# Moving ScalarE's high parts, tanh and gate exponential ahead of its reads of the round's own units

## Chip, cores and metric

The kernel runs on one core of a Trainium2 chip. The metric is device time in microseconds of one execution; lower is better. Times come from runs on the chip, and the trace from one further, profiled execution.

## What is computed

The input `x` has 8 sequences of 512 tokens with 256 features. After a layer norm (`xn`), three branches are computed and all are added to `x`:

```python
xn = layernorm(x)
# branch 1: state-space block
u  = causal_conv4(xn @ W_in + b_in)          # depthwise, 4 taps, 512 channels
ys = scan(h = tanh(A) h + u_t Bp;  y = Cp h + Dp u_t)
r1 = silu(ys) @ W_out + b_out
# branch 2: attention, 16 heads of 16, softmax over 512 keys
r2 = softmax(q k^T / 4) v
# branch 3: mixture of 8 experts, the two largest gates
r3 = sum_e combine_e * (xn @ W_e + b_e)
out = x + r1 + r2 + r3
```

The scan is linear and the same for every channel, so the kernel replaces it with a product along time by a Toeplitz matrix of the impulse response (`Rh`, `Rl`), done ahead of `W_in`. `silu(y)` is computed as `y/2 * (1 + tanh(y/2))`.

## The kernel before, in words

**Numbers in two parts.** Every matrix product is made of single-pass fp32r operands. A value is split into a high part, which ScalarE writes (a copy that rounds to fp32r), and a low part, which VectorE or GpSimd writes as value minus high part. A product is then three matmuls: high by high, low by high, high by low (`three`, L464).

**Rounds.** The main loop has one round `t` for each score tile: 256 rounds with scores (8 sequences, 4 groups of heads each, 8 tiles a group), and 16 more to drain. In round t:

- TensorE (`@block.tensor`, loop at its end) does `score(t)` (L591) into `SB`; `turned(t - 11)` (L608), the transposed scores, into `TB`; in each fourth round `values(m)` (L624); and then the units that the planner gave to this round (`AT[t]`).
- VectorE does `largest(t)` (L1051), the row maximum of `SB`; then the convolution taps (`conv`, L897 for the first tap and L901 for the other three); then the low parts of the units that are read in this round; then `(tanh + 1) * ys` (L1086); then a few gate steps and layer-norm steps (`xn`, L1027).
- ScalarE does the exponential of `TB` (L830), and reads the units out of PSUM.
- GpSimd adds the results in `mt` to `acc` (L1118) and makes the low parts `yl` (L1239) and `xl` (L1216).

`score(t)` waits for `largest(t - 1)`, since there is one `SB`. Each engine runs its own list in the order in which it is written; semaphores alone join the lists.

**Units.** A unit is a batch of matmuls into one of three PSUM banks (`FB`): T transposes `xn`, V makes values and gate logits, Q makes queries and keys, Z is the Toeplitz product, Y is the product with `W_in`, M is an expert product, O is the product with `W_out`, C and X are small transposes, P transposes the attention output for the normalisation. `plan()` sets the order when the kernel is built, from a table of TensorE costs (`COST`), a table of VectorE work (`VECTOR`) and due times (`WANTED`). All engines follow that plan. Of the units that TensorE computes in round t, the last is read by the other engines at the beginning of round t + 1 (`early(t + 1)`), and all others at the end of round t itself (`late(t)`). A bank is taken again three units later, when both reads of it are over.

**ScalarE's round.** The list of ScalarE (`@block.scalar`, the loop over t from -1) is: reads of `early(t)`, the exponential of `TB`, every eighth round a copy of the attention output, reads of `late(t)`, and then these four items, when the round has them:

```python
for b, d in y_read(t - 6): y_hi(b, d)     # L761: yh <- th
for b, d in y_read(t - 4): tanh(b, d)     # L753: th <- ys
x_hi(b, t - XH[b])                        # L767: xh <- xn
G[:, 1] = exp(G[:, 0])                    # L870: the gate's exponential
```

Their waits are: `y_hi` for L1086 of the round before, and for an O unit of the sequence before; `tanh` for all four taps of its convolution (the last tap is done by VectorE in this same round t, right behind `largest(t)`) and for `yl` of the Y unit before, on GpSimd, since `th` is one buffer; `x_hi` for its part of `xn`; the gate's exponential for a subtraction on GpSimd. The four items are 32 + 32 + 32 + 8 = 104 instructions in the whole program.

VectorE's list in round t has the low part of a unit in `late(t)` right behind the taps: for a Q unit `qkl` (L927) waits until ScalarE has written `qkh` (L704); for a V unit the gate logits (L922) wait until ScalarE has written `V` (L694); for a T unit `xTl` (L914) waits for `xTh` (L690); for an X unit `ml` (L909) waits for `mh` (L685).

Of the kernel before, what the change touches and what calls it, by code (L numbers as in the profile page):

```python
# [9 lines left out]
ACT = mybir.ActivationFunctionType  # L10
AX = mybir.AxisListType

NB = 8
# [158 lines left out]
AT, XH, LN = plan()  # L172
# [13 lines left out]
def gate_at(t, engine):  # L186

    for b in range(NB):
        for name, on, late in GATE:
            if on == engine and UNIT["V", b, 3].t + 1 + late == t:  # L190
                yield b, name


def early(t):

    return AT[t - 1][-1:] if t - 1 in AT else []


def late(t):

    return AT[t][:-1] if t in AT else []
# [7 lines left out]
def gate_count(b, name):  # L209

    mine = [n for n, on, _ in GATE if on == ON[name]]
    return b * len(mine) + mine.index(name) + 1


def y_read(t):

    return [(u.b, u.i) for u in early(t) + late(t) if u.kind == "Y"]


def program(nc, x, wqk, bqk, wqk0, bqk0, wvg, bv, bg, win, bin_, cw, cwt, cb, A, AT_, Bp, Cp, Dp, wout, bout, wexp, bexp, out):  # L220
    ctx = ExitStack()
    with ctx:
        def sb(name, shape, dt=F32):
            return ctx.enter_context(nc.sbuf_tensor(name, shape, dt))

        def sem(name):
            return ctx.enter_context(nc.semaphore(name))
# [72 lines left out]
        G = sb("G", [128, 6, 4, 8])  # L300
# [68 lines left out]
        s_gate = {"DVE": sem("gate_vector"), "POOL": sem("gate_pool"), "ACT": sem("gate_scalar")}  # L369
# [27 lines left out]
        def full(kind, b, i):  # L397
            u = UNIT[kind, b, i]
            return s_full[u.bank], u.use
# [8 lines left out]
        def gate_done(b, name):  # L408
            return s_gate[ON[name]], gate_count(b, name)
# [29 lines left out]
        def shifted_rows(e, k, s):  # L439

            p = (0, 64, 8, 72, 16, 80, 24, 88)[k]
            src = kp[p:p + 1, :]
            e.dma_start(Rraw[16 * k:16 * k + 16, :],
                        bass.AP(src.tensor, src.offset + 128 - 16 * k, [[src.ap[0][0], 1], [-1, 16], [1, 640]])).then_inc(s, 16)
# [7 lines left out]
        def turned_bank(t):  # L452

            return SB if t >= FREE and (t - FREE) % 2 == 0 else TB
# [207 lines left out]
        def _(e):  # L662
            def split(w):
                stg, src, hi, lo, sc = stages[w]
                e.wait_ge(s_w[w], 16)
                e.activation(hi, stg, ACT.Copy, scale=sc).then_inc(s_hi[w], 1)
# [79 lines left out]
            def tanh(b, d):  # L746
                n = 4 * b + d
                e.wait_ge(s_cv, 4 * n + 4)
                if n:
                    e.wait_ge(s_yl, n)  # L750
                else:
                    e.wait_ge(s_kr, 1)
                e.activation(th[:, :], ys[:, d % 2, :], ACT.Tanh, scale=0.5).then_inc(s_th, 1)  # L753

            def y_hi(b, d):
                e.wait_ge(s_y, 4 * b + d + 1)
                if b:
                    e.wait_ge(*full("O", b - 1, d // 2 * 2 + 1))
                elif d == 0:
                    e.wait_ge(*full("B", 0, 3))  # L760
                e.copy(yh[:, d, :], th[:, :]).then_inc(s_yh, 1)  # L761

            def x_hi(b, a):
                e.wait_ge(s_xn, 4 * b + a + 1)
                if b and a == 0:
                    e.wait_ge(*full("Y", b - 1, 3))
                e.copy(xhn[:, a, :], xn[:, a, :]).then_inc(s_xh, 1)  # L767

            def krylov(s):
                P = TB[:, s % 2, :]  # L770
                m = 1 << s
                e.wait_ge(s_kx, s + 1)
                if s < 8:
                    e.copy(Pm[:, (s + 1) % 2, :], P[0:17, 256:290]).then_inc(s_kv, 1)
                e.copy(V0[:, m:2 * m], P[0:17, 0:m]).then_inc(s_kv, 1)

            def at_start(t):
                if t == 0:
                    split(W_E0)
                elif t == 1:  # L780
                    e.wait_ge(s_bw, 2)
                    e.copy(bst, bwr).then_inc(s_wh, 1)
                    split(W_E1)
                elif t == 2:
                    e.wait_ge(s_rr[0], 64)
                    e.wait_ge(s_rr[1], 64)
                    e.copy(Rh[:, :], Rraw).then_inc(s_Rh, 1)
                    e.wait_ge(s_srs, 48)
                    e.copy(sst[0:68, :], sraw).then_inc(s_sh, 1)
                elif t == 3:  # L790
                    split(W_IN)
                elif t == 4:
                    split(W_E2)
                elif t == 5:
                    split(W_E3)
                elif t == 8:
                    e.wait_ge(s_br, 48)
                    e.copy(bhi, braw).then_inc(s_bh, 1)
                elif t == 12:
                    split(W_OUT)  # L800
# [17 lines left out]
            for t in range(-1, END + 1):  # L818
                for u in early(t):
                    unit(u)  # L820
                    for s in KRYLOV.get((u.kind, u.i), ()) if t == 0 else ():
                        krylov(s)
                T = t - LAG
                if 0 <= T < STEPS:
                    e.wait_ge(s_ST, T + 1)
                    if T >= NP:
                        e.wait_ge(s_PV, (T - NP) // 2 + 1)
                    elif T < 3:
                        e.wait_ge(s_lo[(W_Q0, W_VG, W_IN)[T]], 1)
                    e.activation(Pt[:, T % NP, :, :], turned_bank(T)[:, :, :], ACT.Exp, scale=0.25).then_inc(s_ex, 1)  # L830
                g, rest = divmod(t - LAG - 8, 8)
                if rest == 0 and 0 <= g < NG:
                    e.wait_ge(s_PV, 4 * g + 4)
                    if g:
                        e.wait_ge(*full("P", (g - 1) // 4, g - 1))
                    else:
                        e.wait_ge(s_kr, 1)
                    e.copy(ot[:, :], OB[:, :]).then_inc(s_ot, 1)
                for u in late(t):
                    unit(u)  # L840
                    if t == -1:
                        for s in KRYLOV.get((u.kind, u.i), ()):
                            krylov(s)
                        if (u.kind, u.i) == ("T", 1):
                            split(W_VG)
                            split(W_QK)
                    if t == 0 and (u.kind, u.i) == ("V", 0):
                        krylov(8)
                    if t == 0 and (u.kind, u.i) == ("V", 1):
                        e.wait_ge(s_kr, 1)  # L850
                        e.wait_ge(s_id, 3)
                        e.copy(kp[:, 256:768], TB[:, 1, :]).then_inc(s_kp, 1)
                        e.wait_ge(s_kp, 1)
                        e.wait_ge(s_c[C_DP], 16)
                        for p in (slice(0, 32), slice(64, 96)):
                            e.activation(kp[p, 256:257], kp[p, 256:257], ACT.Identity,
                                         bias=dpc[p, :]).then_inc(s_kp, 1)
                        e.wait_ge(s_kp, 3)
                        for k in range(4, 8):
                            shifted_rows(e, k, s_rr[1])  # L860
                for b, d in y_read(t - 6):
                    y_hi(b, d)
                for b, d in y_read(t - 4):
                    tanh(b, d)
                for b in range(NB):
                    if 0 <= t - XH[b] < 4:
                        x_hi(b, t - XH[b])
                for b, name in gate_at(t, "ACT"):
                    e.wait_ge(*gate_done(b, "s"))
                    e.activation(G[:, 1, :, :], G[:, 0, :, :], ACT.Exp).then_inc(s_gate["ACT"], 1)  # L870
                at_start(t)

        @block.vector
# [495 lines left out]
```

## Time and profile before

| what | value |
|---|---|
| median of 3 runs | 788.62 us (787.76 to 788.94) |
| the profiled execution, its own time | 787.89 us |
| span of the profiled execution | 786.1 us |
| time of that execution outside its span | 1.8 us |
| mean granted TensorE clock | 0.994 |
| rounds | 256 with scores, 16 to drain |

Times in the rows below are us from the start of the span. A row of a timeline is: start, length, engine, line, operation, operands, number of instructions merged into it, and in brackets the idle time of the engine just before it with the instruction that ended it. ScalarE is ACT, VectorE is DVE, GpSimd is POOL, TensorE's matmuls are PE and its weight loads PEld.

### The profile page before, as it was taken

The numbers are of one execution on the slowest core, as the hardware profiler recorded it, in microseconds if no ns is written. First come the engines' busy times: TensorE is split into PE (matmuls) and PEld (weight loads), VectorE is DVE, ScalarE is ACT, GpSimd is POOL, SyncE is SP. The second block draws the span as 40 slices with busy tenths as digits, with TensorE's granted clock in tenths as the row PEclk, the third lists the DMA queues.
The fourth block names the chain that finished last, engine by engine and source line by source line (L and its number), as shares of the span: only waits on it lengthen the run. The fifth ranks groups of instructions, "written<-read, shape, count | busy, mean of one in ns | idle before, by whom it ended". The sixth has DMA issues, their size and how long they took to land.

```text
span 786.1 us, 13228 instructions
## 1 busy us (share of the span) xinstructions
PE 753.9 (96%) x4404; PEld 453.3 (58%) x4404; DVE 581.4 (74%) x846; ACT 535.4 (68%) x926; POOL 387.4 (49%) x522
## 2 busy tenths in 40 slices
PE   9689999999998999999999999989999999999996
PEld 7457556565555655556555665556655565555553
DVE  6689876976679875887759876698667987568920
ACT  4637766777666767667567775667666776767775
POOL 8445554455444834456346463445444473435654
PEclk9989999999999999999999999999999999999999
DMA  8301201122110221102111121113111121112000
GB/s 272 69 4 44 68 19 28 38 59 78 35 38 13 79 58 41 42 22 82 35 42 42 45 82 31 38 25 95 42 42 43 32 58 39 46 41 69 23 2 27
DMA packets 32465, 39.09 MB, mean 50 GB/s; under 512 B 8513, under 2 KB 18535, under 8 KB 32398
## 3 DMA queue, kind: packets, MB, share of 16 engines
q1 hardware_dynamic: 31418, 37.29, 18.1%
q10 hardware_dynamic: 980, 0.96, 0.6%
q8 instruction: 35, 0.57, 0.3%
q14 instruction: 32, 0.26, 0.1%
HBM read 8.74 MB, written 4.19 MB: 16 GB/s over the span
## 4 chain that ended last, share of the span: by engine, by line
PE 80%; DVE 13%; issue 4%; ACT 3%; ACTq 0%; DVEq 0%
PE PS L464 39%; PE PS L624 12%; PE SB L591 12%; PE TB L608 7%; PE PS L521 5%; DVE mx L1051 4%; PE PS L480 2%; DVE ys L901 2%; DVE xn L1027 1%; PE PS L631 1%; DVE xl L933 1%; DVE qkl L927 1%; DVE ys L897 1%; PE PS L476 1%; DVE th L1086 1%
## 5 line engine op out<-in xcount | busy, mean ns | idle before, releaser
L1051 DVE TENSOR_REDUCE mx<-SB 128x2 f32<-128x1024 f32 x256 | 312.9, 1222 | 141.0 <-PE SB L591 139.9
L1118 POOL TENSOR_TENSOR acc<-acc,mt 128x256 f32<-128x256 f32 x320 | 247.9, 782 | 251.0 <-ACT mt L675 178.9
L830 ACT ACTIVATE Pt<-TB 128x1024 f32<-128x1024 f32 x251 | 257.7, 1027 | 59.3 <-PE TB L608 56.3
L675 ACT ACTIVATE mt<-PS,cpad 128x256 f32<-128x256 f32 x256 | 107.5, 471 | 58.9 <-PE PS L464 58.5
L591 PE MATMUL SB<-kst,qst 48*128 48x512 f32 x512 | 127.9, 496 | 14.6 <-DVE mx L1051 14.3
L624 PE MATMUL PS<-Pt,V 128*17 128x512 f32 x1024 | 122.3, 595 | 0.0
L591 PEld LDWEIGHTS SB<-kst,qst 48*128 48x128 f32 x512 | 47.7, 183 | 125.3 <-DVE mx L1051 75.1
L464 PE MATMUL PS<-weh,xTh 128*128 128x512 f32 x256 | 109.9, 429 | 2.2 <-DVE xTl L914 1.3
L608 PE MATMUL TB<-qst,kst 50*128 50x512 f32 x502 | 101.2, 398 | 1.1 <-ACT Pt L830 1.0
L464 PE MATMUL PS<-wel,xTh 128*128 128x512 f32 x256 | 100.9, 394 | 0.0
L464 PE MATMUL PS<-weh,xTl 128*128 128x512 f32 x256 | 100.6, 393 | 0.0
L901 DVE SCALAR_TENSOR_TENSOR ys<-uc,cwc,ys 128x511 f32<-128x511 f32 (+2 forms) x96 | 88.3, 919 | 0.0
L464 PEld LDWEIGHTS PS<-weh,xTh 128*128 128x128 f32 x256 | 48.4, 189 | 29.2 <-issue 15.8
L624 PEld LDWEIGHTS PS<-Pt,V 128*17 128x17 f32 x1024 | 23.5, 96 | 62.9 <-issue 62.6
L1239 POOL TENSOR_TENSOR yl<-th,yh 128x512 fp32r<-128x512 f32 x32 | 42.1, 1316 | 32.2 <-ACT yh L761 32.1
L464 PEld LDWEIGHTS PS<-wel,xTh 128*128 128x128 f32 x256 | 48.1, 188 | 11.1
L464 PEld LDWEIGHTS PS<-weh,xTl 128*128 128x128 f32 x256 | 48.4, 189 | 6.9
L608 PEld LDWEIGHTS TB<-qst,kst 50*128 50x128 f32 x502 | 47.7, 187 | 5.5 <-ACT Pt L830 5.0
L1216 POOL TENSOR_TENSOR xl<-xn,xh 128x256 fp32r<-128x256 f32 x32 | 28.8, 906 | 20.6 <-ACT xh L767 20.6
L1127 POOL TENSOR_TENSOR acc<-acc,at 128x256 f32<-128x256 f32 x31 | 24.5, 789 | 29.1 <-DVE at L961 27.7
L464 PE MATMUL PS<-wouth,yh 128*128 128x256 f32 x128 | 37.3, 291 | 0.0
L464 PE MATMUL PS<-woutl,yh 128*128 128x256 f32 x128 | 36.0, 281 | 0.0
(162 smaller groups left out, 1142.6 us busy)
## 6 DMA issues: line engine op xcount, KB each, us to landing
qst<-qkh SPq DMA_DIRECT2D x124, 64.0 KB, 2.3
kst<-qkh SPq DMA_DIRECT2D x124, 64.0 KB, 2.3
out<-acc SPq DMA_DIRECT2D x8, 512.0 KB, 2.8
qst<-qkl SPq DMA_DIRECT2D x62, 64.0 KB, 2.2
kst<-qkl SPq DMA_DIRECT2D x62, 64.0 KB, 2.3
acc<-in_x SPq DMA_DIRECT2D x7, 512.0 KB, 3.9
Bt<-in_wexp SPq DMA_DIRECT2D x2, 512.0 KB, 7.6
raw<-in_wexp SPq DMA_DIRECT2D x2, 512.0 KB, 8.8
```

The lines of the kernel that those rows point to most:

```text
L464: ins = e.matmul(P, u, v, start=(start and k == 0), stop=(stop and k == n - 1))
L521: ins = e.matmul(P[:, lo:lo + n], p[:, c, fs], q[:, r:r + n], start=(k == 0), stop=(k == 11))
L591: ins = e.matmul(SB[:, h, :], qst[rows, g % 3, jj, 128 * a:128 * a + 128], kst[rows, g % 3, jj, :], start=True, stop=True)
L608: ins = e.matmul(turned_bank(t)[:, h, :], kst[rows, g % 3, jj, 128 * a:128 * a + 128], qst[rows, g % 3, jj, :], start=True, stop=True)
L624: ins = e.matmul(OB[32 * j:32 * j + 17, :], V[:, g // 4 % 2, a, 4 * (g % 4) + j, :], Pt[:, (2 * m + j % 2) % NP, j // 2, :], start=(a == 0 ...
L675: return e.activation(mt[:, item % NM, :], P, ACT.Copy, scale=scale)
L830: e.activation(Pt[:, T % NP, :, :], turned_bank(T)[:, :, :], ACT.Exp, scale=0.25).then_inc(s_ex, 1)
L901: ins = e.scalar_tensor_tensor(out=y[:, s:512], in0=v[:, 0:512 - s], scalar=cwc[:, d, 3 - s:4 - s], in1=y[:, s:512], op0=ALU.mult, op1=ALU ...
L1051: e.tensor_reduce(mx[:, g % 2, 0:2, 4 * jj + a], SB[:, :, :], AX.X, ALU.max).then_inc(s_mx, 1)
L1118: e.tensor_tensor(v, v, mt[:, item % NM, :], ALU.add).then_inc(s_mt, 1)
L1216: e.tensor_tensor(xln[:, a, :], xn[:, a, :], F(xhn[:, a, :]), ALU.subtract).then_inc(s_xl, 1)
L1239: e.tensor_tensor(yl[:, d, :], th[:, :], F(yh[:, d, :]), ALU.subtract).then_inc(s_yl, 1)
```

## The change

In the loop of ScalarE the four items move ahead of the reads of `late(t)`. They still stand behind the exponential of `TB` and the copy of the attention output. Nothing is added or taken away; no other engine's list changes, and the plan is the same.

```diff
                     e.copy(ot[:, :], OB[:, :]).then_inc(s_ot, 1)
+                for b, d in y_read(t - 6):
+                    y_hi(b, d)
+                for b, d in y_read(t - 4):
+                    tanh(b, d)
+                for b in range(NB):
+                    if 0 <= t - XH[b] < 4:
+                        x_hi(b, t - XH[b])
+                for b, name in gate_at(t, "ACT"):
+                    e.wait_ge(*gate_done(b, "s"))
+                    e.activation(G[:, 1, :, :], G[:, 0, :, :], ACT.Exp).then_inc(s_gate["ACT"], 1)
                 for u in late(t):
                     unit(u)
...
-                for b, d in y_read(t - 6):
-                    y_hi(b, d)
-                for b, d in y_read(t - 4):
-                    tanh(b, d)
-                for b in range(NB):
-                    if 0 <= t - XH[b] < 4:
-                        x_hi(b, t - XH[b])
-                for b, name in gate_at(t, "ACT"):
-                    e.wait_ge(*gate_done(b, "s"))
-                    e.activation(G[:, 1, :, :], G[:, 0, :, :], ACT.Exp).then_inc(s_gate["ACT"], 1)
                 at_start(t)
```

The order changes only in rounds that have one of the four items and a unit in `late(t)` that ScalarE reads. In the plan these are 40 of the 272 rounds, with 50 of the 104 items: 19 `y_hi`, 13 `tanh`, 16 `x_hi`, 2 exponentials of the gate. The rounds with a `tanh` among them, and what is read late in them:

| round | late units |
|---|---|
| 11 | T1.1 |
| 14, 18, 44 | Y |
| 48 | X, V2.3 |
| 70, 166, 198 | Q2.2, Q5.2, Q6.2 |
| 113, 145, 242 | M |
| 202 | T7.0, T7.1 |
| 206 | V7.0 |

(Q5.2 is unit 2 of kind Q of sequence 5.) Round 13 has `y_hi` and the late units V1.0 and V1.1; round 72 has `y_hi` and X2.8, T3.0; round 208 has `y_hi`, `x_hi` and X6.25, V7.2; round -1 has `x_hi` and the late units T0.0, T0.1, D0.0 to D0.2.

## Rows read from the trace of the kernel before

**Rows 1.** The page's busy times by engine, and its chain by engine.

```profile
PE 753.9 (96%) x4404; PEld 453.3 (58%) x4404; DVE 581.4 (74%) x846; ACT 535.4 (68%) x926; POOL 387.4 (49%) x522
...
PE 80%; DVE 13%; issue 4%; ACT 3%; ACTq 0%; DVEq 0%
```

**Rows 2.** Waits: engine, line, who was waited for: us in total, times, longest.

```profile
PE SB L591 <- DVE mx L1051: 14.3, 23, 1.8
...
PE TB L608 <- ACT Pt L830: 1.0, 2, 0.9
```

**Rows 3.** Timeline around round 70, ScalarE and VectorE.

```profile
242.84 0.69 ACT L704 ACTIVATE qkh<-PS,bq 128x512 fp32r<-128x512 f32 x1 [0.56 <-PE PS L464]
...
243.82 0.63 ACT L753 ACTIVATE th<-ys 128x512 f32<-128x512 f32 x1 [0.29 <-DVE ys L901]
...
243.04 0.74 DVE L901 SCALAR_TENSOR_TENSOR ys<-uc,cwc,ys 128x509 f32<-128x509 f32 x1
```

**Rows 4.** The chain that ended last, its pieces in rounds 70, 166 and 198.

```profile
243.70 0.74 DVE qkl L927
...
522.41 0.06 DVE qkl L927
...
610.48 0.06 DVE qkl L927
```

**Rows 5.** Timeline of ScalarE in round 166.

```profile
521.69 0.69 ACT L704 ACTIVATE qkh<-PS,bq 128x512 fp32r<-128x512 f32 x1 [0.56 <-PE PS L464]
...
523.70 0.63 ACT L753 ACTIVATE th<-ys 128x512 f32<-128x512 f32 x1 [1.33 <-POOL yl L1239]
```

**Rows 6.** Timeline of round 198, ScalarE and VectorE.

```profile
609.76 0.69 ACT L704 ACTIVATE qkh<-PS,bq 128x512 fp32r<-128x512 f32 x1 [0.55 <-PE PS L464]
...
609.55 0.74 DVE L901 SCALAR_TENSOR_TENSOR ys<-uc,cwc,ys 128x509 f32<-128x509 f32 x1
```

**Rows 7.** Timeline of round 202, VectorE, and the chain's piece behind it.

```profile
621.27 0.88 DVE L901 SCALAR_TENSOR_TENSOR ys<-uc,cwc,ys 128x509 f32<-128x509 f32 x1
622.08 1.28 DVE L914 TENSOR_TENSOR xTl<-PS,xTh 128x512 fp32r<-128x512 f32 x2
623.27 1.21 DVE L1051 TENSOR_REDUCE mx<-SB 128x2 f32<-128x1024 f32 x1
...
625.26 0.43 PE SB L591 x2
```

**Rows 8.** Timeline of round 206, ScalarE and VectorE.

```profile
634.26 0.63 ACT L753 ACTIVATE th<-ys 128x512 f32<-128x512 f32 x1 [0.70 <-DVE ys L901]
...
634.15 0.15 DVE L922 TENSOR_TENSOR G<-PS,bgb 128x8 f32<-128x8 f32 x1
```

**Rows 9.** Round 13: timeline of ScalarE, two pieces of the chain; all of `yh`.

```profile
74.88 0.81 ACT L694 COPY V<-PS 128x256 f32<-128x256 f32 x2
...
75.31 0.38 ACT V L694
...
75.88 2.64 DVE woutl L880 x4
...
L761 ACT CAST yh<-th 128x512 fp32r<-128x512 f32 x32 | 19.9, 621 | 0.0
```

**Rows 10.** Timeline of ScalarE in rounds -1 and 2.

```profile
9.87 1.06 ACT L690 CAST xTh<-PS 128x512 fp32r<-128x512 f32 x2
...
32.88 0.40 ACT L767 CAST xh<-xn 128x256 fp32r<-128x256 f32 x1
33.18 0.23 ACT L870 ACTIVATE G<-G 128x32 f32<-128x32 f32 x1
```

**Rows 11.** Timeline of ScalarE in round 113.

```profile
368.96 0.84 ACT L675 ACTIVATE mt<-PS,cpad 128x256 f32<-128x256 f32 x2 [0.56 <-PE PS L464]
```

**Rows 12.** Timeline in round 163, a tap of the convolution and GpSimd beside it.

```profile
510.49 1.13 DVE L901 SCALAR_TENSOR_TENSOR ys<-uc,cwc,ys 128x509 f32<-128x509 f32 x1
...
509.47 1.61 POOL L1118 TENSOR_TENSOR acc<-acc,mt 128x256 f32<-128x256 f32 x2 [2.04 <-ACT mt L675]
```

## The prediction

> **What bounds the kernel now.** I read the page's busy times first. TensorE is busy for 96% of the span, ScalarE for 68%, and the chain that ended last lies on TensorE for 80%, on VectorE for 13% and on ScalarE for 3% [rows 1]. So ScalarE has room on average, and work moved within its round should matter only where another engine waits for it. The reader should see in the waits that TensorE's matmuls hardly ever wait for ScalarE's exponential (1.0 us in two waits), but that they wait 14.3 us for VectorE's row maximum [rows 2]. Next I read the chain in order of time. It runs through TensorE nearly everywhere; it leaves it for stretches in which VectorE has too much to do: the low parts of a Q or T unit, a layer norm and the taps in the same rounds. Three of its pieces are the `qkl` of rounds 70, 166 and 198 [rows 4]: there a VectorE instruction that waits for a read of ScalarE is on the path that sets the end. That is where an order on ScalarE costs or gains.
>
> **What the change does, part by part.** It adds and removes no instruction and no DMA. 54 of the 104 items stand in rounds in which ScalarE reads no late unit, and keep their place. 50 move, in 40 rounds. ScalarE's list is in order, so a read of a late unit now waits for everything that the moved item waits for. I went through all 40 rounds in the timelines of ScalarE and VectorE.
>
> *Rounds with `tanh` ahead of a late Q unit (70, 166, 198).* `tanh` needs the last tap of the convolution, which VectorE makes in the same round, and VectorE's next instruction is the `qkl` that needs ScalarE's `qkh`. Before, `qkh` was made while VectorE was at the row maximum and the tap. Now it comes behind `tanh`, and VectorE stands still for `tanh` plus `qkh`.
> - Round 70: the tap ends at 243.04 + 0.74 = 243.78, and `tanh` starts at 243.82, as before [rows 3]. An instruction of ScalarE begins about 0.10 before the one in front ends (32.88 + 0.40 against 33.18) [rows 10], so `qkh` starts at 243.82 + 0.53 = 244.35 and ends 0.69 later at 245.04. `qkl` starts at 245.07 instead of 243.70 [rows 4]: **+1.37**.
> - Round 166: here `tanh` waits longer, until 523.70, for GpSimd's `yl` [rows 5]. `qkh` then ends at 523.70 + 0.53 + 0.69 = 524.92, `qkl` starts at 524.95 instead of 522.41 [rows 4]: **+2.54**.
> - Round 198: the tap ends at 609.55 + 0.74 = 610.29 [rows 6]. 610.33 + 0.53 + 0.69 = 611.55, so 611.58 instead of 610.48: **+1.10**.
>
> Behind `qkl` on VectorE are `xn` of the next sequence, the row maximum of the next round, the next taps and the next `qkl`; TensorE's next score tile and the T unit wait for those. In each of the three stretches the chain stays on VectorE from that `qkl` until TensorE takes over, so nothing there takes the delay in.
>
> *Round 202, `tanh` ahead of T7.0 and T7.1.* The tap ends at 621.27 + 0.88 = 622.15; `tanh` takes 0.53 and a copy of T some 0.6 (1.06 for two [rows 10]), so `xTl` starts near 623.3 instead of 622.08, and the row maximum of round 203, at 623.27 before, ends at 624.5 + 1.21 = 625.7. The score tile behind it ran at 625.26 [rows 7]: **+0.5**. What lay between was TensorE's `values`.
> *Round 206, `tanh` and `x_hi` ahead of V7.0.* 634.26 + 0.53 + 0.30 + 0.38 = 635.47, so VectorE's gate logits start 1.35 later than 634.15 [rows 8]. The same cover as in round 202 leaves 0.5 of it; round 208, where `mh` comes 0.8 later and an O unit waits for that bank, adds some 0.2: **+0.7**, with bounds 0 and 1.35.
> *Round 13, `y_hi` ahead of V1.0 and V1.1.* `y_hi` takes 0.62 [rows 9], 0.52 to the next start. It begins at 74.88, where V1.0 was read; two reads follow, the second at 74.88 + 0.52 + 0.27 = 75.67 instead of 75.31, a piece of the chain with VectorE's split of `W_out` right behind it: **+0.36**.
> *Round -1, `x_hi` ahead of T0.0.* T0.0 is ready when ScalarE comes free at 9.87, so `x_hi` puts 0.30 ahead of it [rows 10] and of the krylov step behind it, for which TensorE waits before D0.0: **+0.30**. In rounds 0 and 1 `x_hi` falls into a wait for TensorE, or takes the place of one that left: 0.
> *Round 48, `tanh` and `x_hi` ahead of X and V2.3:* both low parts come over 1 us later, but the next row maximum had a wait of its own, and only the bank of M1.8 is late: **+0.15**, bounds 0 and 0.8.
> *Round 72, `y_hi` ahead of X and T3.0.* ScalarE's wait for T3.0 hides the 0.52, but GpSimd's `yl` now starts some 1.5 earlier, and lies beside the start of a tap on VectorE's path. What that costs is shown by a tap of 1.13 beside a GpSimd addition [rows 12] against 0.74 for one alone [rows 3], 0.39 more. I take **+0.30**, bounds -0.39 and +0.39. The Trainium skill (GPSIMD Engine Reference, Specifications) says that GpSimd shares its SBUF interfaces with VectorE and contends with its instructions that have two SBUF inputs. The trace agrees for the taps (1.13 against 0.74). By that rule alone an earlier `yl` could also spare a tap as often as it hits one, and the term would be 0.
>
> *The other 31 rounds: 0.* The late units are M, O, Y or X, or V and T units with a GpSimd-side item ahead. In M, O and Y rounds ScalarE stood idle before the read anyway (0.56 in round 113 [rows 11]); a `y_hi` or an `x_hi` fits into that wait, and a `tanh` puts the read back by at most 0.8. No low part hangs on it, and the bank is taken again three units later. Rounds with `y_hi` ahead of V or T (41, 46, 105, 110, 137, 142, 174) put a low part back by 0.3 to 0.5, but the row maximum behind it waited for TensorE for at least as long, or its own low part came second. Without this cover each would cost up to 0.5. For X units the `max_row` DMAs on SP's queue start up to 1.2 later; their rows are needed by `turned` three rounds on, 7 us later.
>
> **Sum.** 1.37 + 2.54 + 1.10 + 0.50 + 0.70 + 0.36 + 0.30 + 0.15 + 0.30 = 7.32 us on the profiled execution's own 787.89, so **795.2**. That execution stands 0.73 below the median of 788.62; by the median it would be 795.9, which the range holds.
>
> **Rivals.**
> 1. *The delays reach the end only in part (789.8 to 792.5).* TensorE catches up with a late VectorE, or round 166 costs 1.2 as the other Q rounds do, because `yl` on GpSimd meets a shifted round earlier. 787.89 + 1.2 + 1.1 + 1.37 x 0.5 gives 790.9. For it: VectorE is busy for only 74%. Against: the three `qkl` are pieces of the chain [rows 4], and behind them it stays on VectorE. The Trainium skill (Perfetto Trace Analysis, Identifying the Most-Contended Engine) holds that matmul busy time doesn't tell how near TensorE is to its limit and that the weight loads' busy share does. Here the two are 96% and 58%, so by that rule TensorE would have reserves and this rival would gain; but its work is a fixed list of matmuls that runs back to back outside the stretches named, and a late start isn't made up.
> 2. *No difference (787.0 to 790.2).* VectorE's stalls would all lie beside TensorE work. It needs rows 4 to be off the path. Time 788.6 plus the 0.3 and 0.36 of the start: 789.3.
> 3. *Faster (785).* Place: the reads of M, O and Y units. ScalarE fills the 0.56 of waiting before a late unit with `y_hi`, `x_hi` and `tanh` [rows 11], so the read of the round's last unit and the next exponential come up to 0.5 earlier, and TensorE, if it waits for those, starts earlier. 27 rounds without a late low part on the path x 0.5 x a quarter gives 3.4, so 785.2. It decides from the point where TensorE's waits for ScalarE exceed VectorE's; the matmuls wait 1.0 us for the exponential and 14.3 us for the row maximum [rows 2], which speaks against it. That VectorE's taps meet GpSimd less often would be worth 0.39 each [rows 12] and could help it along.
> 4. *More than forecast (797.5 to 801).* The later exponentials in rounds 70, 166 and 198 (0.7 to 1.4 late) reach `turned`, or more taps fall beside `yl` and `xl`: ten more at 0.39 give 799.1.
>
> **How the numbers follow.** Forecast (792.5 to 797.5) 0.62; rival 1, 0.16; rival 4, 0.09; rival 2, 0.08; rival 3, 0.05. A measurement of this kernel can tell 0.2%, or 1.6 us, from no change. The first three cases are slower by more than that: 0.87. Same 0.08, faster 0.05. The range from 790.3 to 798.0 holds the forecast with the bounds of rounds 48, 72, 202 and 206, most of rival 1 and the foot of rival 4; rivals 2 and 3 and what is left of 4 are the 2 in 10 left out.
>
> **What would show each step.** After the change `qkl` of rounds 70, 166 and 198 should be preceded by idle time of VectorE of 1.1 to 2.5 us, put down to ScalarE's `qkh`; the total wait of `qkl` for `qkh` should be 5 us above before, and that of `xTl` and the gate logits up by about 1 each. The busy times stay. GpSimd's waits for `yh` and `xh` shrink, and nobody gains by it. The start should be late by 0.3 at the first score tile and 0.7 after round 15. Wrong would be: a span within 1.6 us of before with these stalls present (rival 2), or the stalls absent, because `tanh` was ready before ScalarE came to it.

## The result, and the profile after

The changed kernel takes 800.15 us (median of 4 runs, 799.15 to 800.92) beside 788.78 us before (787.76 to 789.10): a ratio of 1.0145, 95% interval 1.0134 to 1.0157. The profiled execution took 800.92 us, with a span of 799.1 us, 13.0 longer than the span before. The direction was forecast; the size was not: 11.4 us were lost and 7.3 expected. The profiled execution is the slowest of the four, with a mean granted TensorE clock of 0.986 beside 0.989 and 0.990 in the others, so what its rows add up to (13.0 us) is more than the loss by the medians.

The page of the kernel after, its busy times and the shares of the chain that ended last:

```profile
PE 760.9 (95%) x4404; PEld 457.4 (57%) x4404; DVE 581.8 (73%) x846; ACT 534.6 (67%) x926; POOL 388.3 (49%) x522
...
PE 73%; DVE 16%; issue 5%; ACT 3%; POOL 1%; ACTq 1%; DMA 1%; DVEq 0%; POOLq 0%
```

Its waits (engine, line, who was waited for: us in total, times, longest):

```profile
ACT th L753 <- DVE ys L901: 28.1, 27, 2.5
...
PE SB L591 <- DVE mx L1051: 18.6, 27, 2.0
...
DVE qkl L927 <- ACT qkh L704: 9.1, 9, 2.6
...
ACT th L753 <- POOL yl L1239: 2.6, 1, 2.6
```

and one of them in the kernel before:

```profile
DVE qkl L927 <- ACT qkh L704: 4.2, 8, 0.9
```

The busy times of VectorE, ScalarE and GpSimd are as before [rows 1]; it is waiting that grew, and VectorE's share of the chain went from 13% to 16%. The wait of TensorE's matmuls for the row maximum grew from 14.3 to 18.6 us [rows 2]. `qkl` waits 9.1 us for `qkh`, 4.9 more than the 4.2 before; the forecast had 5. `xTl` waits 1.2 us for `xTh` (no such wait before) and the gate logits 8.9 us for `V` (6.6 before), where about 1 us more each was forecast. TensorE's own busy time is 7.0 us longer for the same 4404 matmuls: part of them ran slowly.

Where the 13.0 us arose is read by lining up the row maxima of the two kernels, round by round; the difference of their starts grows in few places. The table says by how much, beside the forecast's term.

| rounds | growth, us | forecast, us |
|---|---|---|
| up to 69 | 0.47 | 0.81 |
| 70 | 1.36 | 1.37 |
| 71 to 165 | 2.71 (2.54 of it up to round 75) | 0.30 |
| 166 | 1.83 | 2.54 |
| 167 to 197 | -0.05 | 0 |
| 198 | 1.09 | 1.10 |
| 199 to 205 | 0.33 | 0.50 |
| 206 to 210 | 3.51 | 0.70 |
| 211 to 242 | 0.05 | 0 |
| 243 to 252 | 1.71 | 0 |

The timelines of ScalarE and VectorE in the kernel after in rounds 70, 166 and 198 show the mechanism; each `qkl` stands behind a wait for `qkh`, which stands behind `tanh`:

```profile
244.82 1.25 ACT L704 ACTIVATE qkh<-PS,bq 128x512 fp32r<-128x512 f32 x2
...
245.52 0.75 DVE L927 SCALAR_TENSOR_TENSOR qkl<-PS,bq,qkh 128x512 fp32r<-128x512 f32 x1 [1.28 <-ACT qkh L704]
...
528.24 0.63 ACT L753 ACTIVATE th<-ys 128x512 f32<-128x512 f32 x1 [2.55 <-POOL yl L1239]
...
529.48 0.75 DVE L927 SCALAR_TENSOR_TENSOR qkl<-PS,bq,qkh 128x512 fp32r<-128x512 f32 x1 [2.59 <-ACT qkh L704]
...
616.65 0.63 ACT L753 ACTIVATE th<-ys 128x512 f32<-128x512 f32 x1 [1.12 <-DVE ys L901]
...
617.89 0.75 DVE L927 SCALAR_TENSOR_TENSOR qkl<-PS,bq,qkh 128x512 fp32r<-128x512 f32 x1 [1.28 <-ACT qkh L704]
```

The waits of 1.28, 2.59 and 1.28 us were forecast as 1.1 to 2.5. Before, in the same rounds, `qkl` stood right behind the tap [rows 3, 4, 6], in round 198 after a wait of 0.20 us.

**A second cause, TensorE's clock.** Busy times in stretches of 4 us (stretch, length, busy PE, PEld, DVE, ACT, POOL with counts, granted clock of TensorE, DMA share, GB/s), first of the kernel after, round 72 and behind it:

```profile
248.00:252.00 4.00, 2.73 (x15) 1.53 (x17) 4.00 (x8) 2.66 (x5) 1.27 (x1) 0.88 0.02 4
252.00:256.00 4.00, 4.00 (x11) 2.77 (x12) 3.69 (x6) 1.42 (x3) 0.00 (x0) 0.50 0.01 3
256.00:260.00 4.00, 4.00 (x16) 2.79 (x15) 0.00 (x0) 1.66 (x4) 1.03 (x2) 0.77 0.01 3
```

then of the kernel before:

```profile
252.00:256.00 4.00, 4.00 (x19) 2.51 (x17) 1.83 (x4) 1.94 (x5) 1.41 (x2) 1.00 0.02 6
```

Then rows of TensorE's timeline, first of the kernel after:

```profile
248.11 0.50 PE L591 MATMUL SB<-kst,qst 48*128 48x512 f32 x2 [0.96 <-DVE mx L1051]
...
250.35 1.34 PE L487 MATMUL PS<-ident,xn 128*128 128x128 f32 x6 [1.05 <-DVE xn L1027]
...
253.54 0.63 PE L464 MATMUL PS<-xh,winl 128*128 128x512 f32 x1
```

and of the kernel before:

```profile
248.53 1.09 PE L487 MATMUL PS<-ident,xn 128*128 128x128 f32 x6 [0.71 <-DVE xn L1027]
249.98 0.50 PE L591 MATMUL SB<-kst,qst 48*128 48x512 f32 x2 [0.37 <-DVE mx L1051]
```

TensorE waited 0.96 us for the row maximum and 1.05 us for `xn`, and from about 251.0 us its clock was granted at 0.5, which is the lower of its two levels (1.2 instead of 2.4 GHz), for 6.8 us (worked out from the three stretches). A matmul of 512 columns then takes 0.63 us and starts 0.43 behind the last, where at full clock it took 0.40 and started 0.23 behind. That is the growth of 2.25 us from round 73 to round 74, which the forecast did not have. A second fall stands at 648 to 656 us (granted 0.80 and 0.77), behind the stalls of rounds 206 to 209, with a growth of 1.43 us.

Such falls differ from execution to execution of the same order. The four other profiles with round 70's stall and no fill (e1, e4, e7, e15 below) all have the first one too, but half as long, and their growth from round 73 to round 74 is 1.15, 1.32, 0.61 and 1.10 us. The second one stands in one other profile (e3) of the four that have the same order in rounds 202 to 208 (e3, e6, e7, e17).

**A third cause, GpSimd beside VectorE's taps.** Timelines of VectorE and GpSimd in rounds 208 and 244 of the kernel after:

```profile
647.36 1.49 DVE L901 SCALAR_TENSOR_TENSOR ys<-uc,cwc,ys 128x511 f32<-128x511 f32 x1
...
740.61 1.78 DVE L901 SCALAR_TENSOR_TENSOR ys<-uc,cwc,ys 128x511 f32<-128x511 f32 x1
...
647.04 1.27 POOL L1239 TENSOR_TENSOR yl<-th,yh 128x512 fp32r<-128x512 f32 x1 [1.28 <-ACT yh L761]
...
740.57 1.28 POOL L1239 TENSOR_TENSOR yl<-th,yh 128x512 fp32r<-128x512 f32 x1 [1.56 <-ACT yh L761]
```

In the kernel before these two taps took 0.74 and 0.73 us, since `yl` came later than they. Now each ends 0.54 us behind the end of `yl` (647.36 + 1.49 = 648.85 against 647.04 + 1.27 = 648.31, and 742.39 against 741.85). A tap that starts during `yl` is thus not slowed by a share: it cannot end before `yl` is done. The forecast's row shows the same: its tap ended at 511.62, GpSimd's two additions at 509.47 + 1.61 = 511.08 [rows 12]. It is no single case: the trace of the kernel before has 54 taps that start more than 0.2 us before the end of one of GpSimd's additions, `yl` or `xl`, and every one of them ends 0.54 to 0.56 us behind it. Six taps that start beside GpSimd's `rs` (L1225, 128x4, 1.02 us) keep their 0.74. The loss is what is left of `yl` when the tap starts, less 0.2, so up to 1.05 us for a tap that starts with it; 0.39 was one case taken for the price. The Trainium skill (SBUF — State Buffer, Who interferes with whom) says so: a VectorE instruction with two SBUF inputs and a GpSimd instruction that reads SBUF exclude each other, and the one that comes second is blocked. These rows agree with it.

### The profile page after: what moved, and what is told of

Read it like the earlier page. It is cut to its first block, busy times and chain, and to the rows that moved or that the text cites. A ratio compares the mean times of both kernels' runs of the same rounds, so it can differ in the third digit from the quotient of the medians.

```text
span 799.1 us, 13228 instructions
## 1 busy us (share of the span) xinstructions
PE 760.9 (95%) x4404; PEld 457.4 (57%) x4404; DVE 581.8 (73%) x846; ACT 534.6 (67%) x926; POOL 388.3 (49%) x522
## 4 chain that ended last, share of the span: by engine, by line
PE 73%; DVE 16%; issue 5%; ACT 3%; POOL 1%; ACTq 1%; DMA 1%; DVEq 0%; POOLq 0%
PE PS L464 36%; PE PS L624 11%; PE SB L591 11%; DVE mx L1051 6%; PE TB L608 6%; PE PS L521 4%; DVE ys L901 3%; PE PS L480 1%; DVE ys L897 1%; DVE xn L1027 1%; DVE th L1086 1%; DVE xl L933 1%; PE PS L476 1%; DVE qkl L927 1%; ACT qkh L704 1%
## 5 line engine op out<-in xcount | busy, mean ns | idle before, releaser
L591 PE MATMUL SB<-kst,qst 48*128 48x512 f32 x512 | 128.8, 500 | 19.1 <-DVE mx L1051 18.6
L753 ACT ACTIVATE th<-ys 128x512 f32<-128x512 f32 x32 | 20.2, 632 | 30.7 <-DVE ys L901 28.1
```

The source lines that it names most:

```text
L591: ins = e.matmul(SB[:, h, :], qst[rows, g % 3, jj, 128 * a:128 * a + 128], kst[rows, g % 3, jj, :], start=True, stop=True)
```

## The experiments

All experiments have one form: a function `ahead(kind, t)` says for each of the four items (`"y"` for `y_hi`, `"t"` for `tanh`, `"x"` for `x_hi`, `"g"` for the gate's exponential) whether it stands ahead of the late reads of round t or behind them.

```diff
+                if ahead("y", t):
+                    for b, d in y_read(t - 6): y_hi(b, d)
+                if ahead("t", t):
+                    for b, d in y_read(t - 4): tanh(b, d)
...
                 for u in late(t):
                     unit(u)
...
+                if not ahead("y", t):
+                    for b, d in y_read(t - 6): y_hi(b, d)
...
```

Results, each beside runs of the kernel before on the same chip:

| run | median, us | before, us | ratio (95% interval) |
|---|---|---|---|
| e1_tanh_only | 799.99 | 788.96 | 1.0142 (1.0129 to 1.0156) |
| e2_rest_only | 788.69 | 788.96 | 0.9997 (0.9988 to 1.0006) |
| e3_q_back | 794.83 | 788.96 | 1.0084 (1.0069 to 1.0099) |
| e4_only_70 | 791.52 | 788.96 | 1.0037 (1.0023 to 1.0051) |
| e5_qtv_back | 791.70 | 788.76 | 1.0037 (1.0024 to 1.0050) |
| e6_fill_72 | 798.02 | 788.76 | 1.0121 (1.0107 to 1.0135) |
| e7_242_back | 798.96 | 788.76 | 1.0124 (1.0110 to 1.0139) |
| e9_before_fills | 790.66 | 788.76 | 1.0021 (1.0012 to 1.0030) |
| e11_only_206 | 790.74 | 788.75 | 1.0034 (1.0023 to 1.0046) |
| e13_fill8_z | 788.01 | 788.75 | 0.9991 (0.9981 to 1.0002) |
| e14_six_back | 790.26 | 788.75 | 1.0014 (1.0005 to 1.0022) |
| e15_y208_back | 799.50 | 788.75 | 1.0135 (1.0122 to 1.0148) |
| e16_rest_fills | 787.18 | 788.92 | 0.9976 (0.9967 to 0.9985) |
| e17_three_and_y72_back | 794.04 | 788.92 | 1.0067 (1.0054 to 1.0079) |

### Which item it is

e1_tanh_only and e2_rest_only, in this order:

```diff
+def ahead(kind, t): return kind == "t"
```

```diff
+def ahead(kind, t): return kind != "t"
```

> Only tanh moves ahead of the late reads; the high parts and the gate's exponential stay behind them. Theory A (what costs is a late Q, T or V unit whose low part on VectorE waits behind tanh, in rounds 70, 166, 198, 202 and 206, with what TensorE loses behind those stalls): nearly all of the loss stays, ratio to before 1.011 to 1.014. Theory B (the loss comes from high parts that put GpSimd's yl and xl beside VectorE's taps): under 1.005.

> The high parts and the gate's exponential move ahead of the late reads; tanh stays behind them. Theory A: only round -1 (0.3 us), round 13 (0.4 us) and round 72 (up to 0.4 us) are left, 789 to 790, ratio 1.000 to 1.002. Theory B: 795 or more. Rival 3 of the prediction (ScalarE's waits are filled and TensorE gains): under 787.

`tanh` alone gives 799.99 us, the whole loss; the other three alone give 788.69, no difference from before. So the loss comes of 13 moved instructions out of 50, and of those that wait for VectorE. Filling ScalarE's waits with the high parts gained nothing. The rival of GpSimd beside the taps is refuted as the cause by itself, but see below.

### Which rounds

e3_q_back, e5_qtv_back and e14_six_back, in this order:

```diff
+def ahead(kind, t): return not (kind == "t" and t in (70, 166, 198))
```

```diff
+def ahead(kind, t): return not (kind == "t" and t in (70, 166, 198, 202, 206))
```

```diff
+def ahead(kind, t): return not (kind == "t" and t in (70, 166, 198, 202, 206, 242))
```

> The whole change, but in rounds 70, 166 and 198 tanh stays behind the late Q unit. Theory A: the steps of 1.4, 1.8 and 1.1 us at these rounds go, and with round 70's stall the low TensorE clock of rounds 72 to 74 (2.3 us) goes too: 6.6 us less than the changed kernel, 793.5; left are rounds 202 to 210 and 242 to 250. If the low clock came of something else, the row clock stays at 0.5 around 252 us and the time is 796.

> The whole change, but tanh stays behind the late units of rounds 70, 166, 198, 202 and 206 (all that have a late Q, T or V unit but X and V2.3 of round 48). The theory of late reads behind tanh: 3.5 to 4 us less than with only the three Q rounds undone (794.8), so about 791; left are the start (0.3), a low clock in rounds 73 and 74 (1.4) and the steps of rounds 244 to 250 (1.5). The rival, that rounds 206 to 210 are slow because x_hi and y_hi stand ahead: the step of 3.5 us between rounds 206 and 210 stays and the time is 794.

> The whole change, but tanh stays behind the late units of rounds 70, 166, 198, 202, 206 and 242. Theory: with these six of the 104 items back in their places the loss is gone but for the start, rounds 13 and 48 and a low clock in some executions: 789.0 to 790.5. Rival: the loss lies in many small delays over the other 34 rounds; then it stays above 791.

The three Q rounds give back 5.3 us (800.15 to 794.83), the T and V rounds 202 and 206 another 3.1 (to 791.70), round 242 another 1.4 (to 790.26). Six instructions of ScalarE hold 9.9 of the 11.4 us. The steps forecast for e3 had been 6.6; one of them, the low clock behind round 70, did not go in its profile. Of the last 1.5 us the profiled execution shows 0.35 at round 49, 0.20 at round 17 and three steps of 0.36 to 0.62 between rounds 167 and 209, beside low clocks of 0.80 and 0.77 at 520 to 528 us. Its runs fall into two groups: three at 788.4 to 788.7 and eight at 790.1 to 791.3. Their mean granted clocks are 0.993 in the three and 0.991 to 0.994 in the eight, so a low clock in some executions does not by itself separate them. What does, and which of the seven other `tanh` it takes, is left open.

### Round 70 alone, and the clock behind it

```diff
+def ahead(kind, t): return kind == "t" and t == 70
```

> Of the whole change, only tanh of round 70 is moved. Theory A: VectorE's qkl waits 1.3 us for ScalarE there, and the stall also brings the low clock behind it: 788.8 + 1.4 + 2.3 = 792.5. If the stall alone does it and the clock fell for another reason: 790.2. If VectorE's stall is made up later: 788.8.

791.52 us, 2.6 more than before: 1.36 us of growth at round 71 and 1.32 more at round 74, where the granted clock at 252 to 256 us is 0.58. `y_hi` is in its old place here, so round 70's stall is enough for that fall. That is 1.0 less than was expected, as the fall here is shorter than in the kernel after. One moved `tanh` of 0.63 us costs four times its length.

e6_fill_72 is the changed kernel with a fill in TensorE's transpositions of T3.0:

```diff
+                        if b == 3 and i == 0 and a == 2:
+                            for _ in range(8):
+                                e.matmul(P[:, 256:384], ident[:, :], ident[:, :], start=True, stop=True)
                         if i == 0:
                             e.wait_ge(s_xn, 4 * b + a + 1)
```

> The whole change, and eight small matmuls of TensorE in the wait for xn in front of T3.0 (round 72), into the bank that this unit has and overwrites afterwards; nothing of the computation changes. Theory: the low clock around 252 us in the changed kernel comes of TensorE's idle time in rounds 71 and 72; with the wait filled the granted clock stays at its full level in 248 to 260 us, and the 2.3 us step of rounds 72 to 74 shrinks to 0 to 0.6: 798. Rival: the step is not the clock's but the order's, then it stays: 800.

798.02 us, 2.1 less than the changed kernel. Stretches of this kernel, where the fill stands at 250.40 us (columns as above):

```profile
248.00:252.00 4.00, 3.05 (x26) 2.26 (x23) 4.00 (x8) 2.00 (x4) 0.04 (x1) 1.00 0.02 4
252.00:256.00 4.00, 3.71 (x23) 2.68 (x22) 4.00 (x6) 2.42 (x5) 1.23 (x1) 1.00 0.00 1
256.00:260.00 4.00, 4.00 (x21) 2.62 (x20) 1.80 (x3) 2.42 (x6) 2.18 (x3) 1.00 0.02 5
```

The stall of round 70 is there as in the changed kernel (growth 1.37), the clock stays at its full level, and the growth at round 74 is gone. All four runs (797.85 to 798.41) lie under all four of the changed kernel. So the low clock was a cost of its own, set off by TensorE's waits.

In e3 the clock had fallen at the same place (0.57 at 252 to 256 us) although round 70 had no stall, and so it had in e2 (0.71, growth 1.38 at round 74). What was left there was `y_hi` ahead of X2.8 and T3.0 in round 72.

So e17_three_and_y72_back puts that item back too:

```diff
+def ahead(kind, t): return not (kind == "t" and t in (70, 166, 198) or kind == "y" and t == 72)
```

> As the run with the three Q rounds undone (794.8), and y_hi of round 72 stays behind X2.8 and T3.0 too. Theory: there the clock still fell at 252 us without round 70's stall, because yl beside VectorE's tap of round 72 put TensorE's wait over the edge; with y_hi behind, the granted clock at 248 to 260 us stays full, the tap goes back to 0.75, and the time is 793.2 to 793.8. Rival: the clock falls there by something else that the change brings, or at random: 794.8 and a low clock as before.

The tap of round 72 and GpSimd's `yl` in the timelines of e3, and then of e17:

```profile
250.76 0.94 DVE L924 SCALAR_TENSOR_TENSOR ys<-uc,cwc,ys 128x511 f32<-128x511 f32 x1
...
249.88 1.27 POOL L1262 TENSOR_TENSOR yl<-th,yh 128x512 fp32r<-128x512 f32 x1 [5.17 <-ACT yh L766]
```

```profile
251.69 0.75 DVE L924 SCALAR_TENSOR_TENSOR ys<-uc,cwc,ys 128x511 f32<-128x511 f32 x1
```

and the stretch behind it, again e3 and then e17:

```profile
252.00:256.00 4.00, 4.00 (x11) 3.15 (x12) 2.88 (x4) 1.28 (x2) 0.00 (x0) 0.57 0.03 6
```

```profile
252.00:256.00 4.00, 3.90 (x18) 2.61 (x18) 3.61 (x6) 2.45 (x5) 1.34 (x1) 1.00 0.01 3
```

With `y_hi` behind, the tap takes 0.75 instead of 0.94 and the clock stays full. From the row maximum of round 73 to that of round 74 it is 4.63 us in e17, as before the change, and 6.00 in e3: the fall cost 1.4.

That the tap decides it is not shown. e5 has the same order as e3 up to round 198, and in its profile the same tap and the same stretch read:

```profile
251.50 0.94 DVE L924 SCALAR_TENSOR_TENSOR ys<-uc,cwc,ys 128x511 f32<-128x511 f32 x1
```

```profile
252.00:256.00 4.00, 3.70 (x17) 2.48 (x14) 3.63 (x6) 1.83 (x3) 0.00 (x0) 1.00 0.01 3
```

The tap is as long, TensorE's wait for `xn` too (0.76 us, 0.75 in e3), and the clock is full; e14 (tap 0.96) is the same. So with `y_hi` ahead and no stall in round 70 the fall stands in two profiles of four (e2 and e3, not e5 and e14), and with `y_hi` behind in none of four (the kernel before, e11, e13, e17). That fits `y_hi` making the fall possible, but also chance. The medians, 794.04 against 794.83, don't decide it (793.2 to 793.8 was expected): e3's runs lie from 793.95 to 796.85 and e17's from 793.93 to 795.89.

### Rounds 206 to 210

e11_only_206 and e15_y208_back, in this order:

```diff
+def ahead(kind, t): return kind == "t" and t == 206
```

```diff
+def ahead(kind, t): return not (kind == "y" and t == 208)
```

> Of the whole change, only tanh of round 206 is moved, ahead of V7.0. Theory: VectorE's gate logits wait for ScalarE's copy of V7.0 and the row maximum of round 207 comes some 0.9 to 1.2 us late; TensorE's values hide part of it, but VectorE has no idle time up to round 209, so 0.8 to 1.2 us reach the end, and some executions lose 1 to 1.4 us more by a low clock: 789.6 to 790.5. Rival, the forecast's term: 0.5.

> The whole change, but y_hi of round 208 stays behind X6.25 and V7.2. Theory: yl on GpSimd then starts 0.6 us later, and the tap of round 208 on VectorE goes back from 1.49 to 0.74 us, so that the step of 0.7 us at round 209 goes: 799.4, and less where the low clock behind it goes too (798). Rival: the tap is long because of xl, not yl: no change from 800.1.

VectorE and GpSimd in the timelines of e11, rounds 206 to 208:

```profile
635.81 0.17 DVE L945 TENSOR_TENSOR G<-PS,bgb 128x8 f32<-128x8 f32 x1 [0.96 <-ACT V L699]
...
639.98 1.79 DVE L924 SCALAR_TENSOR_TENSOR ys<-uc,cwc,ys 128x511 f32<-128x511 f32 x1
...
639.96 1.27 POOL L1262 TENSOR_TENSOR yl<-th,yh 128x512 fp32r<-128x512 f32 x1 [1.59 <-ACT yh L766]
```

and round 208 in those of e15:

```profile
648.21 0.73 DVE L924 SCALAR_TENSOR_TENSOR ys<-uc,cwc,ys 128x511 f32<-128x511 f32 x1
...
648.51 1.59 POOL L1262 TENSOR_TENSOR yl<-th,yh 128x512 fp32r<-128x512 f32 x1 [1.90 <-ACT yh L766]
```

e11 costs 2.0 us (790.74): 0.91 at round 207 from the wait for V7.0, and 1.03 at round 209 from the tap of 1.79 us, and both are in the end (growth 2.0). That tap (end 641.77, `yl` 641.23, again 0.54 apart) is long although `y_hi` of round 208 is in its old place. `tanh` moved VectorE against GpSimd by one wait, and what had stood one after the other then stood side by side. In e15 `y_hi` behind the late reads lets the tap start first: it takes 0.73 instead of 1.49, and now `yl` is the one that waits (1.59 instead of 1.27); the growths of 0.73 at round 209 and of 1.43 at round 210 are both gone in the profile. Only the first can be put down to the edit: e6, e7 and e17 keep the growth at round 209 (0.74 each) and have none at round 210 either. The median falls by 0.65, to 799.50, which is about the 0.76 us of the tap, though the runs of the two kernels overlap (798.41 to 799.86 against 799.15 to 800.92). The profile of e15 also has a low clock at 532 to 536 us (0.62, growth 1.17 at round 169), which the changed kernel's has not.

### Round 242

e7_242_back:

```diff
+def ahead(kind, t): return not (kind == "t" and t == 242)
```

> The whole change, but tanh of round 242 stays behind M7.2. Theory: there tanh puts two reads of M units back by 0.6 us, GpSimd adds them later, and its work and yl then lie beside VectorE's taps and the product behind tanh in rounds 243 to 249, which take up to 1.8 instead of 0.7 us; with that undone the 1.5 us between rounds 243 and 252 go: 798.6. Rival: yl and the additions lie there because y_hi of rounds 244 and 248 comes early; then 800.

798.96 us, 1.2 less. The tap of round 244 in e7:

```profile
737.52 0.73 DVE L924 SCALAR_TENSOR_TENSOR ys<-uc,cwc,ys 128x511 f32<-128x511 f32 x1
```

It is 0.73 us again, against 1.78, and all of the 1.7 us between rounds 243 and 252 is gone in the profile. All four runs (796.40 to 799.10) lie under all four of the changed kernel. No low part on VectorE waits for M7.2. `tanh` puts two reads of M units back, GpSimd adds them later, and so works beside the product behind `tanh` and the taps.

### Fills at the start, and a faster kernel

The kernel before has a low clock of its own: it waits 3 us ahead of Z0.0 in round 4.

Three runs put matmuls there whose product nobody reads, as e6 did. e9_before_fills is the kernel before with 18 of them and the fill of e6; e13_fill8_z is the kernel before with 8 and no other; e16_rest_fills is e2 with 8 and the fill of e6:

```diff
                 elif u.kind == "Z":
+                    if b == 0 and i == 0:
+                        for _ in range(8):
+                            e.matmul(P[:, 0:128], ident[:, :], ident[:, :], start=True, stop=True)
```

> The kernel before with its own order on ScalarE, and small matmuls in two waits of TensorE: 18 in front of Z0.0 of the first sequence (3.0 us of waiting at 36.6 us) and eight in front of the third transposition of T3.0 (round 72). Nothing of the computation changes. Theory: the granted clock at 36 to 44 us is 0.57 since TensorE has been idle; with the wait filled Z0.0 runs in 2.2 instead of 3.9 us, on the path: 1 to 2 us less than before, 787.3. Rival: what follows Z0.0 waits for VectorE and GpSimd anyway; then no change.

> The kernel before with its own order, and eight small matmuls of TensorE in front of Z0.0 of the first sequence, which waits 3.0 us for GpSimd's xl there. (Eighteen took 5.9 us, longer than the wait.) Theory: they end before xl is there and keep the clock up, Z0.0 runs in 2.2 instead of 3.9 us: 1.0 to 1.7 us less than before, 787.5. Rival: eight at half clock don't keep it up, or the time behind Z0.0 is taken by VectorE anyway: 788.8.

> High parts and the gate's exponential ahead, tanh behind (as in the run that made no difference), with eight small matmuls in front of Z0.0 of the first sequence and eight in the wait of T3.0. Theory: the clock stays at its full level around 252 us and for most of Z0.0, and what the fills save (1 us at the start, 1.4 us where the low clock fell around 252 us) reaches the end: 786.5 to 787.5, a little under both kernels. Rival: the clock falls later instead (as at 520 us in other runs) and nothing is gained: 788.7.

e9 was a miss: 790.66, 1.9 more than before. A row of TensorE's timeline in it says why, and the same row of e13 follows:

```profile
36.78 5.91 PE L523 MATMUL PS<-ident 128*128 128x128 f32 x36
```

```profile
37.40 2.80 PE L520 MATMUL PS<-ident 128*128 128x128 f32 x16
```

Eighteen fills took 5.9 us, twice the wait. (Each of these fp32 matmuls is recorded as two.) Eight took 2.8 and fitted. The profile of e9 loses 0.9 us at round 5, right behind the fills, and 1.0 more at round 167, beside a low clock of 0.72 at 520 to 524 us. e13 gives 788.01, whose interval still reaches to no difference, and its runs spread from 786.2 to 790.4. e16, with both fills and the high parts ahead, gives **787.18 us**, 0.24% under the kernel before (0.15 to 0.33%), and so beats both. Its stretches at the start, and then those of the kernel before:

```profile
36.00:40.00 4.00, 3.99 (x19) 3.55 (x20) 3.90 (x5) 0.12 (x1) 4.00 (x3) 0.57 0.34 80
40.00:44.00 4.00, 4.00 (x24) 3.35 (x23) 3.47 (x5) 0.00 (x0) 1.54 (x3) 1.00 0.07 16
```

```profile
36.00:40.00 4.00, 0.95 (x3) 0.67 (x4) 3.93 (x5) 0.46 (x1) 4.00 (x3) 0.58 0.42 98
40.00:44.00 4.00, 4.00 (x15) 3.24 (x15) 2.35 (x5) 0.00 (x0) 1.54 (x3) 0.56 0.00 0
```

At 40 to 44 us the clock is granted in full instead of at 0.56, and round 5 comes 1.4 us earlier. Which of the two fills, and whether the high parts help, no run here separates with certainty.

## Why the prediction was right or wrong, point by point

By the rows of the profiled execution, 13.0 us arose where the sum had 7.3. Three steps failed. The term of rounds 206 to 210 was mis-sized (3.51 us for 0.70). TensorE's clock behind round 70's stall had no term at all (the 2.71 us of rounds 71 to 165, for 0.30). And the "other 31 rounds: 0" left out round 242 (1.71). Together they are 6.9 us too little; round 166 (0.71), the start (0.34) and round 202 (0.17) were 1.2 us too much together.

**What bounds, and the mechanism: right.** ScalarE's order costs where a VectorE instruction on the path waits for the read. e1 and e2 show that it is `tanh`, and e3, e5 and e14 that it is the rounds named. Rival 3 (faster) is refuted by e2, and rivals 1 and 2 by the growths: that of round 70 still stands in round 165, and that of round 166 in round 197.

**Rounds 70 and 198: right** (1.36 and 1.09 measured, 1.37 and 1.10 forecast).

**Round 166: stall right, net 0.7 too high.** `qkl` waited 2.59 us and came 2.53 later, as worked out. But the row maximum behind it came only 1.83 later: the two `xn` between them took 1.43 us before, beside GpSimd's `yl` (until 523.61 us) and its additions, and 0.73 after, when GpSimd was done before they began.

**Round 202: right** (0.5 forecast, growth of 0.63 from round 202 to 205).

**Rounds 206 to 210: the step that failed in its size.** The forecast let TensorE's `values` hide all but 0.5 of the wait of 1.35, and gave 0.2 to `mh`. In fact VectorE had no idle time from that wait to the row maximum of round 209, so the 1.2 us stayed (0.91 by e11, with `tanh` alone); the tap of round 208 took 1.49 instead of 0.74, since `yl` was beside it (e15 takes that away); and TensorE waited for the bank of X6.25, upon which its clock fell (1.43). The row of TensorE's timeline:

```profile
649.10 0.38 PE L555 MATMUL PS<-be,cT 72*128 72x256 f32 x1 [0.86 <-DVE ml L909]
```

That makes 3.51 against 0.70. Without the fall, as in e6, e7 and e17, it is 2.06. The cause of the first two parts is shown; why the clock fell in some executions and not in others is open.

**Rounds 70 to 74: the second that failed.** The tap of round 72 beside `yl` was there (0.94 in e3 against 0.75 in e17), for 0.2 us. What was left out is TensorE's clock behind the stall of round 70: 2.25 us in the profile, 2.1 by e6, 1.3 in e4. The page had shown the means to see it: the kernel before runs at a granted clock of 0.58 and 0.56 at 36 to 44 us, behind a wait of TensorE, and the prediction never asked which of the new waits would do the same.

**"The other 31 rounds: 0": wrong for round 242** (1.2 us by e7). The forecast asked who waits for a late read on VectorE, and did not follow the M units to GpSimd. The mechanism stood in the prediction as rival 4, with ten taps at 0.39 each; the number of taps was too high there and the price of one too low, as up to 1.05 is lost by one that starts with `yl`.

**Rounds -1, 13 and 48.** The 0.30 of round -1 is not seen: the first row maximum came 0.06 us earlier than before. The runs cannot size it either, since the first row maximum of ten profiles with `x_hi` ahead there lies 0.42 earlier to 0.96 later than in the kernel before, and that of five with it behind (e1, e4, e9, e11, e13) 0.18 to 0.89 later. Round 48 has 0.34 instead of 0.15, within its bounds. The 0.36 of round 13 did not come. In round 13 the gate logits came late as worked out, but GpSimd's `yl` also came earlier (75.95 instead of 76.28), and VectorE's split of `W_out` beside it took 2.27 instead of 2.72 us. Round 14 came at 78.45, against 78.44.

**The range.** 800.15 lies beyond its upper end of 798.0. Rival 4, the only case above, had 0.09 and named taps, not the clock.

## What to carry to other kernels

In an in-order list, an item may be moved ahead of a read only if everything that it waits for is there before the read is: here an item that waits for an engine (`tanh` for VectorE's tap) stood ahead of one that the same engine needs next. Whoever prices such a stall has to add two things behind it: what the shift brings side by side on engines that slow each other down, and whether the engine with the clock now has waits behind which it may be given a lower one. A few matmuls without use in such a wait, no longer than the wait, can keep it (e6, e16); eighteen of them, twice as long as the wait, cost more than they saved (e9).

## What the runs showed of the hardware that was not expected

- TensorE's granted clock fell to its lower level after waits of 0.96 and 1.05 us, where the kernel before had 0.71 and 0.37 and kept it. What a fall costs ranges widely: 2.25 us at round 74 of the kernel after, 0.6 to 1.4 there in e1 to e4, e7 and e15, and nothing in e6, whose clock was at 0.91 and 0.66 from 520 to 528 us while the growth did not move.
- The same order with the same waits can keep the clock in one execution and lose it in another: 0.57 in e3 and 1.00 in e5 at 252 to 256 us.
- A tap that starts during one of GpSimd's additions, `yl` or `xl`, more than 0.2 us before its end, ends 0.54 to 0.56 us behind it: 54 times in the kernel before, and in the kernel after twice, e11 and e3 with starts from 0.02 to 0.88 us apart. The row maximum out of PSUM keeps its length (1.19 to 1.23 us) in the whole kernel.
